# Transposing two feature columns at a time in a recommendation tower kernel

## The reference, cut to what matters

```python
e = jnp.stack([tbl_0[ids[:, 0]], ..., tbl_25[ids[:, 25]]], axis=1)          # (2048, 26, 128)
combined = jnp.concatenate([dense[:, None, :], e], axis=1)                  # (2048, 27, 128)
interactions = jnp.einsum('bfd,bgd->bfg', combined, combined)
iu, ju = jnp.triu_indices(27, k=1)
z = jnp.concatenate([dense, interactions[:, iu, ju]], axis=1)
h = jnp.concatenate([z, dense], axis=1)                                     # (2048, 607)
h = jnp.maximum(h @ W_top1 + b_top1, 0.0)                                   # 512 wide
h = jnp.maximum(h @ W_top2 + b_top2, 0.0)                                   # 256 wide
y = h @ W_top3
```

## Time and profile before

| | |
|---|---|
| median of 3 runs | 523.08 us |
| the profiled execution's own time | 513.81 us |
| its span on the core | 512.0 us |
| mean granted TensorE clock | 0.917 of full speed |
| TensorE products / weight loads busy | 408.9 us / 362.6 us |
| VectorE / ScalarE / GpSimd busy | 245.8 / 136.1 / 263.1 us |

### The profile page before, as it was taken

The page is one execution under the profiler, slowest core; times in us unless marked ns, Lnnn a source line. Parts: engine busy times, 40 slices in busy tenths (PEclk is TensorE's granted clock), DMA queues, the critical chain, the costliest instruction groups (busy, mean ns, idle before and its releaser), DMA issues.

```text
span 512.0 us, 10047 instructions
## 1 busy us (share of the span) xinstructions
PE 408.9 (80%) x4352; PEld 362.6 (71%) x4352; DVE 245.8 (48%) x312; ACT 136.1 (27%) x356; POOL 263.1 (51%) x280
## 2 busy tenths in 40 slices
PE   2885387857979688879878799797887968887998
PEld 2664366746867578768867678686776857886976
DVE  5994127554445454446453454545543454433332
ACT  2451112321223222223212322233212222123531
POOL 6787464552556636454635646264463654635000
PEclk9997596978999799998989979898998979989999
DMA  7978112221212212221212212123121221211000
GB/s 197 249 187 258 36 47 67 70 67 42 63 42 86 84 33 65 61 87 49 68 43 72 73 53 68 37 83 83 49 57 52 70 65 49 57 32 53 3 12 1
DMA packets 20133, 36.74 MB, mean 72 GB/s; under 512 B 6157, under 2 KB 9877, under 8 KB 20090
## 3 DMA queue, kind: packets, MB, share of 16 engines
q0 software_dynamic: 8704, 17.84, 12.7%
q1 hardware_dynamic: 5338, 9.08, 6.8%
q10 hardware_dynamic: 6048, 9.18, 5.9%
HBM read 36.07 MB, written 0.01 MB: 70 GB/s over the span
## 4 chain that ended last, share of the span: by engine, by line
PE 61%; another core or an unknown queue 13%; issue 12%; DVE 10%; ACT 2%; DMA 1%; SPq 0%; ACTq 0%; DVEq 0%
PE psB L382 23%; PE psG L408 14%; DVE one_hot L646 7%; PE psB L453 7%; PE psB L366 5%; PE psB L460 4%; PE psB L418 2%; PE psB L447 2%; DVE tab_lo L651 2%; PE psB L432 2%; DMA ET<-tbl 1%; PE psB L465 1%; DVE ZH L510 1%; ACT ET L553 1%
## 5 line engine op out<-in xcount | busy, mean ns | idle before, releaser
L307 POOL DMA_INDIRECT E<-tbl,gidx x272 | 262.3, 964 | 206.7 <-PE psB L366 109.7
L646 DVE TENSOR_TENSOR one_hot<-oidx,psR 125x1024 fp32r<-125x1024 int32 (+1 forms) x152 | 179.2, 1189 | 116.3 <-remote 60.4
L382 PE MATMUL psB<-one_hot,tab_hi 125*128 125x256 f32 x592 | 117.9, 321 | 19.0 <-ACT tab_hi L535 9.4
L408 PE MATMUL psG<-ET 128*52 128x52 f32 x2048 | 81.9, 228 | 44.4 <-issue 35.7
L382 PE MATMUL psB<-one_hot,tab_lo 125*128 125x256 f32 x592 | 105.4, 302 | 5.6 <-issue 4.7
L408 PEld LDWEIGHTS psG<-ET 128*52 128x52 f32 x2048 | 67.8, 139 | 59.2 <-issue 54.5
L382 PEld LDWEIGHTS psB<-one_hot,tab_hi 125*128 125x128 f32 x592 | 88.4, 206 | 27.3 <-issue 20.5
L382 PEld LDWEIGHTS psB<-one_hot,tab_lo 125*128 125x128 f32 x592 | 90.1, 208 | 9.1 <-issue 7.5
L669 DVE COPY_PREDICATED S<-second,psG 116x208 f32<-116x208 int32 x64 | 25.0, 391 | 103.1 <-ACT S L582 94.0
L582 ACT COPY S<-psG 116x208 f32<-116x208 f32 x64 | 21.2, 333 | 146.6 <-remote 82.0
L553 ACT COPY ET<-psB 128x512 f32<-128x512 f32 (+3 forms) x80 | 44.3, 572 | 50.9 <-PE psB L366 30.9
(11 more groups left out here) (46 smaller groups left out, 188.7 us busy)
## 6 DMA issues: line engine op xcount, KB each, us to landing
oidx<-hot_idx ACTq DMA_DIRECT2D x28, 256.0 KB
E<-tbl,gidx POOLq DMA_INDIRECT x272
ET<-tbl SPq DMA_DIRECT2D x3, 448.0 KB
oidx<-hot_idx SPq DMA_DIRECT2D x4, 256.0 KB
dense<-dense_pairs SPq DMA_DIRECT2D x8, 128.0 KB
ZH<-tbl SPq DMA_DIRECT2D x2, 448.0 KB
S<-tbl SPq DMA_DIRECT2D x2, 448.0 KB
oidx<-hot_idx ACTq DMA_DIRECT2D x7, 128.0 KB
```

Of the source, the lines that this page charges most:

```text
L307: nc.gpsimd.indirect_dma_start(E[:, n % SLOTS, i, :], None, gathered[feature_and_tile(n, i)[0]], bass.IndirectOffsetOnAxis(ap=gidx[:, 4 * ...
L382: product = nc.tensor.matmul(bank[:, t % 2 * DUO:(t % 2 + 1) * DUO], tab[0:ROWS_P, TABLE_BASE[t] + k0 + i, :], one_hot[0:ROWS_P, m % RING, ...
L408: gram = nc.tensor.matmul(psG[g % 2][q * LANE:q * LANE + M, a * M:(a + 1) * M], two[:, 0:M], two[:, PAIR:], start=True, stop=True)
L646: nc.vector.tensor_tensor(one_hot[0:ROWS_P, m % RING, 0:many], ids, rows, ALU.is_equal).then_inc(hot_full[m % RING], 1)
```

## The change

`C` steps take two columns at a time: a slice of `S` of 116 by 128 is turned, and one column lies on the lower 64 partitions of the result, the other on the upper 64. For that `S` is laid out as side, column, position. 13 turns instead of 26 stand in four `C` steps instead of seven. The copies into `U` then bring both columns of a pair side by side on 128 partitions, so that 128 rows of `U` hold all positions up to column 22 but two blocks (`FIRST_BLOCKS`). The blocks of `LAST_BLOCKS` go to 64 further rows for each of the two sides, side by side on the free axis, with a copy for each side and zeros across. `split` has two steps: the first turns 128 by 128 four times and gives both sides at once, the second is four plain float32 products with `stacked` (two identities, one above the other) as the moving operand. `Zp_hi` and `Zp_lo` are written by two instructions each, of 512 and 256 columns, and `U` is cleared once by VectorE behind the weights' split, for which ScalarE waits.

```diff
+    LATE = 4
     KP = 3
     PAIRS = KP * P
-    COLUMNS = [range(c, min(c + 4, F)) for c in range(1, F, 4)]
-    BLOCKS = [range(1, 3), range(3, 5)] + COLUMNS[1:]
+    TWOS = (F - 1) // 2
+    EARLY = TWOS - LATE // 2
+    COLUMNS = [range(t, min(t + 4, EARLY)) for t in range(0, EARLY, 4)] + [range(EARLY, TWOS)]
+    FIRST_BLOCKS = [(0, 1), (1, 2), (2, 4), (4, 5), (6, 8), (8, 10), (10, 11)]
+    LAST_BLOCKS = [(11, 13), (5, 6)]
...
     def splits(d):
-        return [("split", d, kp) for kp in range(KP)]
+        return [("split", d, i) for i in range(2)]
...
-        S = sb("S", [P, F - 1, 2, DUO_J], f32)
+        S = sb("S", [P, 2, F - 1, DUO_J], f32)
-        U = ZH[:, M1 * DUO:M1 * DUO + GROUP * PAIRS].rearrange("p (v r) -> p v r", v=GROUP)
+        U = ZH[:, M1 * DUO:M1 * DUO + GROUP * 2 * P].rearrange("p (v r) -> p v r", v=GROUP)
...
-                for i, c in enumerate(COLUMNS[b]):
-                    turned = nc.tensor.transpose(bank[0:DUO_J, i * P:i * P + MT], S[0:MT, c - 1, d % 2, :],
-                                                 ident[0:MT, 0:MT])
+                for i, t in enumerate(COLUMNS[b]):
+                    two = S[0:MT, d % 2, 2 * t:2 * t + 2, :].rearrange("p f j -> p (f j)")
+                    turned = nc.tensor.transpose(bank[:, i * P:i * P + MT], two, ident[0:MT, 0:MT])
                 turned.then_inc(full, 1)
 
-            def turn_pairs(d, kp):
-                if kp == 0:
+            def turn_pairs(d, i):
+                if i == 0:
                     last = {}
                     for b in range(len(COLUMNS)):
                         bank, used, _ = PLACE["C", d, b]
                         last[bank] = used + 1
                     for bank, count in last.items():
                         pe.wait_ge(bank_out[bank], count)
-                bank, full = wait_empty(pe, ("split", d, kp))
+                bank, full = wait_empty(pe, ("split", d, i))
                 for v in range(GROUP):
-                    turned = nc.tensor.transpose(bank[:, v * DUO_J:(v + 1) * DUO_J],
-                                                 U[0:DUO_J, v, kp * P:(kp + 1) * P], ident[0:DUO_J, 0:DUO_J])
+                    if i == 0:
+                        turned = nc.tensor.transpose(bank[:, v * P:(v + 1) * P], U[:, v, 0:P], ident[:, :])
+                        continue
+                    turned = nc.tensor.matmul(bank[:, v * DUO_J:(v + 1) * DUO_J], U[:, v, P:], stacked[:, :],
+                                              start=True, stop=True)
...
-            for block in BLOCKS:
-                if block[0] not in COLUMNS[b]:
-                    continue
-                n, high, base = len(block), block[-1], block_base[block]
-                at = block[0] - COLUMNS[b][0]
-                turned = bank[0:DUO_J, at * P:(at + n) * P].rearrange(
-                    "p (c h f s) -> p h s f c", c=n, h=2, s=PAIR)[:, :, :, 0:high]
-                rows = U[0:DUO_J, :, base:base + n * high].rearrange("p (h s) (f c) -> p h s f c", h=2, c=n)
-                copied = nc.scalar.copy(rows, turned) if eng is nc.scalar else nc.vector.tensor_copy(rows, turned)
+            def copy(sides, low, high, base):
+                at, n = low - COLUMNS[b][0], high - low
+                turned = bank[sides, at * P:(at + n) * P].rearrange(
+                    "p (t h f s) -> p h s t f", t=n, h=2, s=PAIR)[:, :, :, :, 0:2 * high]
+                rows = U[sides, :, base:base + n * 2 * high].rearrange("p (h s) (t f) -> p h s t f", h=2, t=n)
+                return nc.scalar.copy(rows, turned) if eng is nc.scalar else nc.vector.tensor_copy(rows, turned)
+            for low, high in FIRST_BLOCKS:
+                if low in COLUMNS[b]:
+                    copied = copy(slice(0, P), low, high, block_base[low, high])
+            for low, high in LAST_BLOCKS:
+                if low in COLUMNS[b]:
+                    copy(slice(0, DUO_J), low, high, block_base[low, high])
+                    copied = copy(slice(DUO_J, P), low, high, block_base[low, high] + DUO_J)
...
-        def pairs_as_rows(d, kp):
-            return psB[PLACE["split", d, kp][0]][:, 0:DUO]
+        def pairs_as_rows(d, i):
+            bank = psB[PLACE["split", d, i][0]]
+            if i == 0:
+                return bank[:, :].rearrange("p (v k j) -> p k v j", v=GROUP, k=2)
+            return bank[:, 0:DUO].rearrange("p (k v j) -> p k v j", k=1, v=GROUP)
+        def rows_of(split, i):
+            return split[:, 0:2 if i == 0 else KP].rearrange("p k (v j) -> p k v j", v=GROUP)[:, 2 * i:]
...
-                nc.scalar.copy(Zp_hi[:, kp, :], pairs_as_rows(d, kp)).then_inc(Zp_hi_ready, 1)
+                nc.scalar.copy(rows_of(Zp_hi, i), pairs_as_rows(d, i)).then_inc(Zp_hi_ready, 1)
...
-                    act.wait_ge(w1d_lo_ready, 1)
-                    act.wait_ge(w1_lo_ready, 1)
+                    act.wait_ge(U_cleared, 1)
...
+                dve.wait_ge(w1_lo_ready, 1)
+                dve.wait_ge(w1d_lo_ready, 1)
+                nc.vector.memset(U[:, :, :], 0.0).then_inc(U_cleared, 1)
+                dve.wait_ge(U_cleared, 1)
...
-                split = nc.vector.tensor_tensor(Zp_lo[:, kp, :], pairs_as_rows(d, kp),
-                                                Zp_hi[:, kp, :].bitcast(f32), ALU.subtract)
-                split.then_inc(bank_out[PLACE["split", d, kp][0]], 1)
+                dve.wait_ge(Zp_hi_ready, 2 * d + i + 1)
+                split = nc.vector.tensor_tensor(rows_of(Zp_lo, i), pairs_as_rows(d, i),
+                                                rows_of(Zp_hi, i).bitcast(f32), ALU.subtract)
+                split.then_inc(bank_out[PLACE["split", d, i][0]], 1)
...
+            nc.vector.tensor_tensor(stacked[:, :], ident[:, 0:DUO_J], ident[:, DUO_J:],
+                                    ALU.add).then_inc(stacked_ready, 1)
```

More of the change, by code:

```diff
@@ L450, in perceptron_part @@
                         if p == 0:
-                            wait_out(pe, ("split", d, kp))
+                            wait_out(pe, ("split", d, kp // 2))
                         for w, z in ((w1p_hi, Zp_hi), (w1p_hi, Zp_lo), (w1p_lo, Zp_hi)):
@@ L469, in _ @@
             pe.wait_ge(ident_ready, 1)
+            pe.wait_ge(stacked_ready, 1)
             for h in HALVES:
```

52 lines of the change are left out of this document (32 added, 20 removed).

## The result

The kernel after the change takes **534.56 us** (533.15 to 536.88, 4 runs); beside it, on the same chip, the kernel before took 522.42 us (521.62 to 524.66, 4 runs). The ratio is 1.036 with an interval of 1.028 to 1.045. I had forecast 511.4 us in a range of 500 to 522.5: the time moved the other way and lies outside. The profiled execution of the change took 534.46 us.

The account below looks back on a forecast made before the run. TensorE was taken to bound the kernel, partly by work, partly by late signals. Terms -7.5 - 0.35 + 1.0 + 4.9 - 9.7 = -11.7 us took 523.1 to 511.4 us, range 500 to 522.5.

Parts of the forecast that it names:

- Work, -7.5 us: TensorE's column turns and splits: 2.33 us a duo instead of 3.41, counted over seven duos, -7.5 us.
- The split's wait for VectorE, +4.9 us: First split step waits 0.7 us for VectorE's copies, which stand behind a one-hot chunk, in seven duos: +4.9 us.
- The bank waits, -9.7 us: TensorE's 19.3 us idle ahead of column turns, mostly for PSUM banks: half taken as gained, -9.7 us.
- The last duo, -0.35 us: At the end, the split starts 0.6 us sooner, less 0.25 us for `Zp_lo` in larger pieces: -0.35 us.
- the clear, +1.0 us: At the start, VectorE clears 1024 columns of `U`, all of it on the path: +1.0 us.
- The waits move whole: Rival: waits ahead of the column turns reappear ahead of the split, nothing gained from banks; 521.1 us, chance 0.19.
- The slower rival: VectorE reaches the copies one chunk later, so the split waits 1.92 us in seven duos; 529.7 us, chance 0.11.

Follow-up runs that it names:

- e2_four: The changed kernel with its four column steps at every other of the seven places in the earlier kernel's order: 528.51 us, 1.016 times the kernel before.
- e4_swap: The changed kernel with the copies of C1 and C3 on ScalarE and those of C0 and C2 on VectorE: 530.15 us, no ratio given.
- e3_before: The kernel before, with its 26 single-column turns and three splits, put in the changed kernel's step order: 528.35 us, 1.021 times the kernel before.

## Why the prediction was wrong

**Work, -7.5 us: the turns right, one record mis-sized.** The 13 turns take 1.29 us in the last duo (forecast 1.30). The second split step takes 121 ns a record, where I had taken 74 ns from the old split, as the row that loads as many columns. That gives 2.70 us a duo instead of 2.33, and -5.0 us instead of -7.5 over seven duos. Here the rule that I set aside was nearer: by the Trainium skill, "TensorE: Matmul & The Clock Gate", section "LDWEIGHTS (loading the stationary operand)", a load of 128 columns takes 107 ns. The trace is above even that for the plain products (121 ns), and below it for the transposes that stream 64 and 116 columns (74 and 99 ns). My row was of another kind of instruction, a transpose, and its weights had 64 rows instead of 128; which of the two makes the difference no run separates.

**The split's wait for VectorE, +4.9 us: right by itself.** 0.7 us a duo forecast; 0.74 with the gathers held, and an estimate of about 0.75 on the chip without late signals. The copies' prices (196, 282, 201, 372 ns for forecasts of 190, 280, 200, 360) held too.

**The bank waits, -9.7 us: this step failed.** I wrote that the reason for most of the idle time was gone and took half of it as gained. Nothing of it was: for a forecast of -4.8 us with the term above, 22.5 us ahead of columns and splits became 25.2 (+2.7), and 24 to 35 in the variants with the new products and no filler. `e2_four` shows it most plainly: 1.4 us ahead of the columns, 33.6 ahead of the split, and no gain. I had read myself in the earlier trace rows that the copies start late because signals do, not because a bank is short, and yet counted the bank wait as the cause. TensorE waited wherever it next needed a late copy; taking away one such place moved the wait to the next one, and the nameless waits of all engines together stayed at 284 us.

**Left out: the clock.** The old waits stood in several places, the new ones in one ahead of the split, up to 6.5 us long, and behind it TensorE spends 50.3 us at 1.2 GHz instead of 26.1. In the profiles there are 47.8 us more at half clock in all (+18.4 us of time, as an estimate), in the medians of the timed runs 0.875 against 0.89 to 0.90 of full speed (some +9 us). Nowhere had I priced a moved wait by the clock behind it. The runs with filler show the connection with the idle stretch: work put there removes most of the half clock behind it. They do not show that this alone makes the loss.

**What the miss is made of.** Forecast -11.7 us, measured +12.1: 23.8 us apart. As an estimate, 2.5 of it is work, 7.5 the waits ahead of columns and split (-4.8 forecast, +2.7 measured), 9 the clock at the median, and 4.7 idle time ahead of the turns of gathered tiles, of which I had no term.

**The last duo, -0.35 us, and the clear, +1.0 us.** The memset took 0.91 us (forecast 1.0). In the last duo, 2.83 us lie between the start of the turns' loads and the split (513.82 to 516.65), before 3.23 (494.77 to 498.00): 0.40 less for a forecast of 0.6. But from the split to the first product of `Zp` it is 2.33 us after 1.92, 0.41 more for a forecast of 0.25, which takes that back. In this profile 3.4 us of layer one then run at half clock (519.0 to 522.4), where the kernel before has none, and the stretch from the split to the end is 2.0 us longer.

**The rivals.** "The waits move whole" had the mechanism, at 521.1 us and a chance of 0.19; with the record at its measured price (+2.5) and the lower clock (some +9) it gives 532.6, against 534.6 measured. The slower rival named VectorE's place in its order, and `e4_swap` refutes that. I had also named what would make me wrong (idle ahead of the split over 20 us, plain products over 100 ns), and both came true. The sum failed because it took half of a wait as gained that had only another place to go.

**What stays open** is what makes signals late on four of the chips and not on one; why half of the added time at half clock lies elsewhere than behind the split; and through what the order alone costs 8 us with the old products (`e3_before`). Its accounts (span 525.9 us, clock 0.896, 19.2 us ahead of columns and splits) do not say.

## What to carry to other kernels

A wait whose end is set by a late signal is not removed with the instruction that happens to stand behind it: count it as moved to the next instruction that needs the same engines, and count as gained only what is shown to have another cause. When waits of TensorE are gathered in one place, look at the granted clock behind it and give it a term of its own: here half clock behind the splits went from 26 to 50 us. And price an instruction by a row of its own kind: a plain float32 product by another plain one, not by a transpose of the same shape.

## What the hardware showed unexpectedly

- The same kernel took 384 us on one chip and 520 to 527 us on the others, with equal instruction times at full clock; no engine waited there for a nameless release, against 238 to 334 us in the profiles from the others. A ratio taken on one chip may not hold on another: 1.2% to 3.5% for the same two kernels in two jobs.
- Plain float32 products with 128 columns of weights and 64 streamed: 121 ns a record; turns of 128 by 116: 99 ns; 16 records of 64 by 64: 34 ns each.
- Turns of the identity added to a kernel cost 109 ns each on the chip without late signals (from 12 to 24: 10.5 us for 96; from 24 to 48: 20.9 us for 192), but between nothing and 12.3 us for 192 of them on the others.
